# Values by pair of exponentials, one score and one shift moved, in a small attention kernel on one core

## What is computed

```
x = x + _L0_conv_ref(_gn(x), L0_conv_log_A, L0_conv_dt_w, L0_conv_dt_b, L0_conv_ln_w, L0_conv_ln_b)
t = _to_tokens(x)
t = t + _L1_attn_ref(_ln_t(t), L1_attn_w_qkv, L1_attn_w_out, L1_attn_b_out)
t = t + _L1_ffn_ref(_ln_t(t))
x = _from_tokens(t, x)

attn = jnp.einsum('bhqd,bhkd->bhqk', q, k) / math.sqrt(hd)
bias = jnp.where(pos <= 0, pos.astype(jnp.float32) * math.log(RECENCY_DECAY), jnp.zeros((), dtype=jnp.float32))
attn = jax.nn.softmax(attn + bias[None, None, :, :], axis=-1)
out = jnp.einsum('bhqk,bhkd->bqhd', attn, v).reshape(batch, seq_len, hidden)
return jnp.einsum('bsh,oh->bso', out, w_out) + b_out
```

## Time and profile before

| | |
|---|---|
| time, median of 3 runs | 55.11 us (53.56, 55.11, 55.13) |
| the profiled execution | 53.42 us, its span 51.7 us |
| mean granted TensorE clock | 0.967 of full speed |
| busy PE / DVE / ACT / POOL | 40.9 / 40.2 / 28.6 / 23.5 us |
| costliest group on VectorE | L761, 16 reductions, 10.7 us |
| costliest group on ScalarE | L511, 8 exponentials, 8.0 us |

### The profile page before, as it was taken

How to read it: one execution, slowest core, us unless ns; L and a number is a source line. 1 busy time by engine, 2 the same in 40 slices (tenths; PEclk the granted TensorE clock), 3 DMA queues, 4 the chain that set the end, 5 groups by cost and what they waited for, 6 DMA issues and landing times.

```text
span 51.7 us, 1021 instructions
## 1 busy us (share of the span) xinstructions
PE 40.9 (79%) x310; PEld 26.3 (51%) x312; DVE 40.2 (78%) x135; ACT 28.6 (55%) x63; POOL 23.5 (45%) x64
## 2 busy tenths in 40 slices
PE   0999899999996859649957996999994596996700
PEld 0332789685442645429824682599482352842500
DVE  2799778848983599999889999989999954699520
ACT  3600656395476768967998079339649900056020
POOL 4789432099999989736950031040029204016000
PEclk9999995569999999999999999999999999999999
DMA  0392400000000000000000000000000000002002
GB/s 0 80 304 42 35 5 0 0 0 0 0 0 6 0 0 0 0 6 13 6 0 0 0 0 0 0 13 0 0 0 0 0 0 0 0 0 101 1 0 101
DMA packets 1565, 0.92 MB, mean 18 GB/s; under 512 B 404, under 2 KB 1560, under 8 KB 1560
## 3 DMA queue, kind: packets, MB, share of 16 engines
q1 hardware_dynamic: 1104, 0.79, 4.9%
q10 hardware_dynamic: 456, 0.08, 1.7%
HBM read 0.60 MB, written 0.26 MB: 17 GB/s over the span
## 4 chain that ended last, share of the span: by engine, by line
PE 35%; DVE 24%; POOL 13%; ACT 10%; issue 7%; DMA 6%; POOLq 0%; DVEq 0%
PE ps L1013 8%; ACT probs L511 8%; DMA x_sb<-in_x_dram 6%; PE ps L994 5%; PE ps L963 4%; POOL stacks L303 4%; DVE negmax L761 4%; POOL stacks L304 4%; PE ps L996 4%; PE ps L935 3%; PE ps L1029 3%; PE ps L859 2%; POOL parts L310 2%; PE ps L913 2%; POOL wc L298 2%
## 5 line engine op out<-in xcount | busy, mean ns | idle before, releaser
L761 DVE TENSOR_REDUCE negmax<-ps 128x2 f32<-128x512 f32 x16 | 10.7, 675 | 0.8 <-PE ps L963 0.6
L511 ACT ACTIVATE probs<-ps 128x1024 f32<-128x1024 f32 x8 | 8.0, 1021 | 3.9 <-PE ps L996 3.9
L833 PE MATMUL ps<-warm 128*128 128x512 bf16 x28 | 8.9, 452 | 1.4 <-DVE warm L556 1.3
L994 PE MATMUL ps<-stacks 128*128 128x256 f16 x32 | 7.0, 273 | 0.0
L352 POOL TENSOR_TENSOR on<-pvq,rsum 128x256 f32<-128x256 f32 x3 | 1.8, 616 | 10.7 <-DVE rsum L683 10.7
L996 PE MATMUL ps<-qmk,ident 128*128 128x256 f16 (+1 forms) x32 | 6.6, 246 | 0.0
L963 PE MATMUL ps<-stacks 128*128 128x256 f16 x32 | 6.0, 274 | 0.2 <-ACT stacks L485 0.2
L833 PEld LDWEIGHTS ps<-warm 128*128 128x128 bf16 x30 | 3.2, 113 | 5.0 <-issue 2.2
L1013 PE MATMUL ps<-probs,v_aug 128*32 128x256 f32 x64 | 4.3, 384 | 1.7 <-ACT probs L511 1.5
L913 PE MATMUL ps<-wT,xtT 128*128 128x384 f32 x8 | 3.2, 505 | 0.7 <-ACT xtT L437 0.6
L994 PEld LDWEIGHTS ps<-stacks 128*128 128x128 f16 x32 | 3.1, 98 | 0.8 <-ACT stacks L492 0.4
(11 more groups left out here) (159 smaller groups left out, 94.4 us busy)
## 6 DMA issues: line engine op xcount, KB each, us to landing
x_sb<-in_x_dram SPq DMA_DIRECT2D x1, 256.0 KB, 2.9
out_dram<-y_sb SPq DMA_DIRECT2D x2, 128.0 KB, 1.7
wqkv_sb<-in_L_attn_w_qkv_dram SPq DMA_DIRECT2D x1, 192.0 KB, 3.0
wout_sb<-in_L_attn_w_out_dram SPq DMA_DIRECT2D x1, 64.0 KB, 3.3
bout_bc<-in_L_attn_b_out_dram ACTq DMA_DIRECT2D x1, 64.0 KB, 3.8
params<-in_L_conv_ln_w_dram ACTq DMA_DIRECT2D x1, 1.0 KB
params<-in_L_conv_ln_b_dram ACTq DMA_DIRECT2D x1, 1.0 KB
params<-in_L_conv_dt_w_dram ACTq DMA_DIRECT2D x1, 0.5 KB
```

The lines of the kernel that those rows point to most:

```text
L511: act.activation(probs[:, 2 * c:2 * c + 2, :, :].rearrange("p h k q -> p (h k q)"), s2_ps[c % 2].rearrange("p a n -> p (a n)"), ACT.Exp, s ...
L761: dve.tensor_reduce(negmax[:, g, :, quadrant], s1_ps[h % 2].rearrange("p (q k) -> p q k", q=HALVES), AX_X, ALU.max, negate=True).then_inc( ...
L833: pe.matmul(ps[:, bank, :], warm[:, 0:P], warm[:], start=True, stop=True)
L994: pe.matmul(dst, kT[:, e, HW * b + P * t:HW * b + P * (t + 1)], qT[:, e, HW * b:HW * (b + 1)], start=True, stop=False)
```

## The change

`values(g, t)` becomes `values(g, c)`: it takes the two heads of exponential c of the group, with both tiles of keys, and waits only for that exponential. On TensorE, score 14 moves ahead of the values of group 1, shift 3 ahead of the first projection, and the second half of values of group 2 behind the scores by key of heads 12 to 15; the warm matmuls there go ahead of the whole second projection and are three, not five. The odd shift of group 2 moves from VectorE to ScalarE. On VectorE, transpose `by_dim(1)` moves behind `largest(15)`, `find_channels(0)` ahead of `by_query(2)`, and `by_dim(2)` behind `invert(3)`. On ScalarE, `token_scale(0)` moves behind the last exponential. On GpSimd, the hot fields of batch 0 move ahead of `on` 2 and its three small steps behind `on` 3.

```diff
-WARM_X, WARM_Z, WARM_SCAN, WARM_PV, WARM_OUT = 9, 1, 5, 5, 7
+WARM_X, WARM_Z, WARM_SCAN, WARM_PV, WARM_OUT = 9, 1, 5, 3, 7
...
-            for g in range(NG - 1):
+            for g in range(NG):
+                if g == NG - 2:
+                    hot_fields(0)
                 pool.wait_ge(s_rsum, g + 1)
...
+            def odd_shifts(g):
+                act.wait_ge(s_mT, g + 1)
+                act.copy(qT.rearrange("p (a e) t -> p a e t", e=2)[0:P // 2, 2 * (g % 2):2 * (g % 2) + 2, 1,
+                                                                      HW * (g // 2):HW * (g // 2 + 1)],
+                         mT_ps[0:P // 2, :].unsqueeze(1).broadcast_to([P // 2, 2, HW])).then_inc(s_mro, 1)
...
                 even_shifts(g)
-                if g == NG - 1:
-                    token_scale(0)
+                if g == 2:
+                    odd_shifts(g)
                 exponentials(2 * g)
                 exponentials(2 * g + 1)
+            token_scale(0)
             plus_normalised(0)
...
             by_dim(0)
-            odd_shifts(2)
             largest(13)
+            largest(14)
             by_query(1)
             invert(1)
-            largest(14)
+            largest(15)
             by_dim(1)
-            largest(15)
             residual(0)
             odd_shifts(3)
             token_stats(0)
+            dve.wait_ge(s_consts, 9)
+            find_channels(0)
             by_query(2)
             invert(2)
-            dve.wait_ge(s_consts, 9)
-            find_channels(0)
-            by_dim(2)
             look_up(0)
             by_query(3)
             invert(3)
+            by_dim(2)
             by_dim(3)
...
-            def values(g, t):
+            def values(g, c):
...
+                pe.wait_ge(s_exp, 2 * g + c + 1)
+                for t in range(HALVES):
+                    for j in range(2 * c, 2 * c + 2):
+                        last = pe.matmul(pv_ps[g][VW * j:VW * (j + 1), :],
+                                         v_aug[:, 2 * b + t, HG * (g % 2) + j, :], probs[:, HG * g + j, t, :],
+                                         start=(t == 0), stop=(t == HALVES - 1))
+                if c == 1:
                     last.then_inc(s_pv, 1)
...
+            scores_by_query(12)
+            shift_rows(2)
+            scores_by_query(13)
+            scores_by_query(14)
+            values(1, 0)
+            values(1, 1)
+            scores_by_key(8)
+            scores_by_key(9)
+            scores_by_query(15)
+            scores_by_key(10)
+            scores_by_key(11)
+            shift_rows(3)
             project(0)
-            shift_rows(3)
             values(2, 0)
-            values(2, 1)
             for h in range(HG * (NG - 1), HG * NG):
                 scores_by_key(h)
+            values(2, 1)
             values(3, 0)
             values(3, 1)
+            keep_warm(WARM_PV, 2)
             project(1, [0])
-            keep_warm(WARM_PV, 2)
             project(1, [1])
```

More of the change, by code:

```diff
@@ L348, in _, with hot_fields @@
                     pool.tensor_tensor(t1b[:, t, :], t1[:, t, :], bout_bc[:], ALU.add).then_inc(s_t1b, 1)
-            for g in range(NG - 1):
+            def hot_fields(b):
+                ts = slice(HALVES * b, HALVES * (b + 1))
+                pool.wait_ge(s_above, b + 1)
+                link(pool.tensor_scalar(lift[:, ts], above[:, ts, SHL], 0.5, 0.5, ALU.mult, ALU.add))
+                pool.tensor_tensor(hot[:, ts, :, :], hot_at[:].unsqueeze(1).broadcast_to([P, HALVES, 2, D]),
+                                   lift[:, ts].unsqueeze(2).unsqueeze(3).broadcast_to([P, HALVES, 2, D]), ALU.mult)\
+                    .then_inc(s_hot, 1)
+            for g in range(NG):
+                if g == NG - 2:
+                    hot_fields(0)
                 pool.wait_ge(s_rsum, g + 1)
@@ L357, in _ @@
                 ts = slice(HALVES * b, HALVES * (b + 1))
[L358 to L362, removed]
                 pool.wait_ge(s_frs, b + 1)
@@ L366, in _ @@
                 pool.tensor_tensor(neg_fm[:, ts], fmv[:, ts, 0], neg_frs[:, ts], ALU.mult).then_inc(s_nfm, 1)
[L367 to L371, removed]
+                if b == 1:
+                    hot_fields(b)
         @block.scalar
@@ L998, in scores_by_key @@
                     last.then_inc(s_s2, 1)
-            def values(g, t):
+            def values(g, c):
                 b = g // 2
[L1003 to L1016, removed]
+                if c == 0:
+                    if g == NG - 1:
+                        pe.wait_ge(s_mre, NG)
+                        pe.wait_ge(s_mro, NG)
+                    elif g > 0:
+                        pe.wait_ge(s_pvq, g)
+                    else:
+                        pe.wait_ge(s_odd, NG - 1)
+                        pe.wait_ge(s_even, NG - 1)
+                pe.wait_ge(s_exp, 2 * g + c + 1)
[5 more added lines that the diff above has]
+                if c == 1:
                     last.then_inc(s_pv, 1)
@@ L1086, in _ @@
             scores_by_key(3)
[L1087 to L1098, removed]
+            scores_by_query(8)
+            shift_rows(1)
+            scores_by_query(9)
+            values(0, 0)
+            values(0, 1)
+            scores_by_query(10)
+            scores_by_key(4)
+            scores_by_key(5)
+            scores_by_query(11)
+            scores_by_key(6)
+            scores_by_key(7)
+            scores_by_query(12)
[10 more added lines that the diff above has]
+            shift_rows(3)
             project(0)
-            shift_rows(3)
             values(2, 0)
-            values(2, 1)
             for h in range(HG * (NG - 1), HG * NG):
                 scores_by_key(h)
+            values(2, 1)
             values(3, 0)
             values(3, 1)
+            keep_warm(WARM_PV, 2)
             project(1, [0])
-            keep_warm(WARM_PV, 2)
             project(1, [1])
```

## The result

The changed kernel is slower by 1.5%: the ratio to the kernel before is 1.0153, with a 95% interval of 1.0117 to 1.0188. That is inside 2% and inside the range given, but it is about six times the +0.13 us of the sum: on 53.5 us it is 0.8 us.

What follows compares the result with a forecast made beforehand. A chain of waits to the transpose at 41.87 was taken as the bound. VectorE's 0.34 us gain less the hold put it at 42.0: +0.13 us, 53.55 (median 55.2, chance 0.5). Range 52.9 to 55.6.

Steps and rivals of the forecast that it cites:

- Step 1: TensorE, score 14 ahead of values 1: goes at 32.2, exponential 4 starts at 34.4; worth nothing.
- Step 2: Odd shift 2 moved from VectorE to ScalarE: takes 0.58 us, ready about 33.25, hidden by 0.5 us.
- Step 3: VectorE up to the last score: reduction 15 from 34.6 instead of 35.17; transpose `oT` 1 behind it, 35.6 to 36.05.
- Step 4: TensorE's projection 0 waits for `oT` 1: result at 37.0 against 36.35, residual 0 starts 0.65 us later, at 37.04.
- Step 5: TensorE's half values take half of 1.06 us; exponential 6 at 38.5, values 3 done at 41.2 against 41.77: 0.6 us gained.
- Step 6: VectorE behind the residual: `find_channels(0)` 1.8 us, last transpose at 41.53; gain 0.34 us without anything else, set by VectorE.
- Step 7: GpSimd's product `on` 2 holds VectorE's `val` until it ends (other reading: slowing per element): transpose at 42.0, 0.13 later than before.
- Step 8: Remaining moves (`oT` 2, `token_scale(0)`, `hot_fields(0)`, GpSimd's small steps, two warm matmuls fewer) cost nothing; cover includes 0.43 us idle.
- The stall of the projection: Rival: projection 0 stalls longer, start estimates off by 0.3 together, with the hold: 53.85, median 55.5; chance 0.12.
- The granted clock: Rival: TensorE's clock falls to half in the tail, from 42 us on: +1.7 us, 55.1, median 56.8; chance 0.05.
- Not held: Rival: `val` too small or ahead of GpSimd's product, so no hold: -0.34 us, 53.1, median 54.8; chance 0.25.
- the values set it: Rival: `find_channels(0)` 0.3 us or more faster, nothing held, transpose at 41.2: -0.67 us, 52.75, median 54.4; chance 0.08.

Runs made afterwards that it cites:

- One line: Kernel before with only VectorE's transpose oT 1 (`by_dim(1)`) moved behind reduction 15 (`largest(15)`): ratio 1.0115.
- the kernel with whole values: Changed kernel with each group's values whole again, group 2 whole ahead of the scores by key of heads 12 to 15: ratio 1.0101.
- the start: Kernel before with only score 14 ahead of values 1, odd shift 2 on ScalarE, oT 1 behind reduction 15, shift 3 ahead of projection 0: ratio 1.0102.
- the start undone: Changed kernel with score 14, odd shift 2, oT 1 and shift 3 put back as before, the tail staying changed: ratio 0.9987.

## Why the prediction was right or wrong

The range held the result, and so did the forecast of less than 2% of change, with the likeliest case slightly slower. Neither says much: the range is 2.7 us wide and 2% are 1.1 us, so both held a miss of six times the sum. That part is luck, not a sum that came out. The likeliest case's own range, 55.0 to 55.4 us on the median, was missed (54.33). The size was 0.8 us, not 0.13, and of the steps some held and one failed.

- *Step 1, score 14.* Nearly. It went at 32.42, on before's scale 32.27: TensorE starts 0.14 behind the reduction's end, where I had put 0.07. Exponential 4 was 0.1 us later than before on that scale, not 0.06 earlier.
- *Step 2, odd shift.* Right. 0.58 us in ScalarE's idle time.
- *Step 3, reduction 15.* Right in kind, 0.2 off: 34.94, on before's scale 34.79, for 34.6.
- *Step 4, projection 0.* Right in kind, and it is the main loss. Residual 0 at 37.44, on before's scale 37.29, for 37.04. The delay of the residual that I priced at 0.65 was 0.9; 0.2 of the difference is the later reduction of step 3, which the transpose follows. One line brings 0.58 us at the end by itself.
- *Step 5, halves of values.* **This is the step that failed.** "Half of 1.06 us from 36.9 to 37.4": it took 0.99 us, from 37.33 to 38.32. I divided a group's duration by its pieces, but the four heads write to four stripes of 32 columns and run at the same time; two heads leave two stripes empty and take as long. So exponential 6 came at 39.30, on before's scale 39.15, not 38.5 (0.28 of the difference stood already where the half began), and the second half, another 1.0 us behind head 15's scores, kept `pvq` 2 waiting until 41.13 for a foreseen 40.3. The half behind exponential 7, priced at 0.6, took 1.0 as well: the way from there to the transpose shrank from 1.34 us to 1.15, so of the "0.6 us on this side" that were to pay for step 4 there came 0.19, and the exponentials before it were 0.56 later. What this step makes of the miss can be estimated from the kernel with whole values, whose VectorE was through at 42.31, hold included: with halves at their foreseen price the transpose of the change would have stood near 42.3 instead of 42.76. That is some 0.45 of the 0.61 us between the foreseen 42.0 and the measured 42.61 on before's scale.
- *Step 6, VectorE behind the residual.* Half right. VectorE set the start of the last transpose, but not its own pace up to there: `find_channels(0)` took 1.67 for 1.8, and VectorE idled 0.50 us ahead of `pvq` 2, for the values of step 5.
- *Step 7, the hold.* Right, and in its first reading: an operation on two elements was lengthened from 0.16 to 0.57, and ended 0.01 behind the product. Slowing per element is ruled out. Its price was 0.36 and 0.37 us by two pairs of kernels, where the sum had 0.47 between the two readings. The Trainium skill ("SBUF — State Buffer", section "Who interferes with whom") has a lock that blocks the later of the two for the other's whole instruction; these 0.57 us agree with it.
- *Step 8, the rest.* Right, it cost nothing: output 0's part and the warm matmuls behind it were 0.2 us later against the transpose than before, and 0.20 of the 0.43 us of idle time behind them were left.
- *Rivals.* The stall of the projection, given 0.12, came nearest: it named the right place and 53.85 us, and without step 5 was too small for the 54.29 measured. The granted clock was 1.00 from 12 us on. "Not held" and "the values set it" did not happen.

Do the losses add up? By the ratios the start seems to cost 0.5 us with the tail of before and 0.9 with the tail of the change. The distances show no such thing: it costs 0.51 us in the one case and 0.53 in the other, and in both another 0.1 ahead of exponential 4. The tail alone adds 0.10, and 0.51 + 0.10 is 0.61 of the 0.63 us of the whole change. The rest of the 0.9 lies within the intervals and in the landing of the input, 0.22 us later in the trace of the change than in that with the start undone. Open is how much of the measured 1.5% is such scatter: the traces account for 0.74 us of the 0.8.

## What to carry to other kernels

Before splitting a block of matmuls to start half of it earlier, look where its parts lie in TensorE: here parts in different column stripes already ran together, so half the block took the whole time, and the split paid only where both halves stayed adjacent or the first filled idle time. When a transpose or copy is moved behind a faster producer, follow its other consumer as well: here a reduction came 0.4 us earlier, the residual behind the projection 0.9 later, and the last transpose 0.5 to 0.6 later. When an operation of VectorE releases one of GpSimd, look which small operations with two SBUF inputs stand right behind it on VectorE, and move them in front or away.

## What the runs showed of the hardware

A group of values of four heads took 1.07 us, of two heads 1.06, and of two adjacent halves 1.08; four pieces start together in the first, two in the second, and both take four steps. The Trainium skill ("TensorE: Matmul & The Clock Gate", section "The mechanism" of Part 3) has tiles at different positions overlap, which is the same behaviour seen from the other side; the prediction did not draw on it for this price.

A two-element operation of 0.16 us on VectorE took 0.57 in the three kernels in which it started 0.06 or 0.07 us behind the start of a GpSimd product of 0.61 or 0.62 us (the change, with whole values, and with the start undone), and 0.16 in the eight others. `raised`, with 82 elements, took 0.56 in the four kernels that have it 0.15 or 0.16 us behind the start of that product, and 0.24 or 0.25 in the others. In these cases the length of a hold followed what was left of GpSimd's instruction, not the size of VectorE's.
